# Query weights by GpSimd, one DMA for the repeated rows, and token scales broadcast without a transpose

## The chip, the cores and the metric

The kernel runs on one core of one Trainium2 chip. The metric is device time in microseconds (us), the median over runs, lower is better. The engines are named as the profile names them: PE (TensorE matmul), PEld (TensorE weight load), DVE (VectorE), ACT (ScalarE), POOL (GpSimd) and SP (SyncE, which here only issues DMAs).

## The reference, cut to what matters

64 images of 3x224x224 are cut into 64 patches of 28x28 each and projected to 128 channels; a class token and 128 text tokens are put beside them, so that a sample has L = 193 tokens of 128 channels. One attention layer and one mixture-of-experts layer follow:

```python
h = tokens(x) ++ txt                                     # 64 x 193 x 128
u = layernorm(h)
qkv = group_norm(u @ W_qkv) * scale + bias               # 8 heads, q 8, k 8, v 16 channels
logits = q.k + q.rpe_k + k.rpe_q                         # rpe: relative position, [d, i, j]
attn = softmax(logits)
h = h + group_norm(attn.v + attn.rpe_v) * scale + bias
y = layernorm(h)
top_p = two largest of softmax(y @ Wg), normalised       # 8 experts, no selection of experts
for i in range(2):                                       # every expert runs on every token
    out += sum_e gelu((y * top_p[i]) @ W1[e] + b1[e]) @ W2[e] + sum(b2)
```

The expert layer multiplies each token's hidden row by top_p[0] once and by top_p[1] once. The kernel computes `z = (y*p1) @ W1` for 32 chunks of 128 hidden units, gets the second branch as z times the ratio of the two gates, and adds the two gelus before the product with W2.

## The kernel before, in words

**Stages.** `patch_embed` writes the patch tokens to DRAM. `fused_block` then works on 32 pairs of samples (both samples side by side, T2 = 386 columns). Every engine runs the same list of steps, `SCHEDULE`, once per turn of a loop, and each engine does its own part of a step. One turn holds three pairs at once: the expert layer of pair n (32 steps `c`, of which the first three stand at the end of the turn before as `a`), the attention of pair n+1 ("late" steps), and the first norms and projections of pair n+2 (the steps in `EARLY`, up to `gaff`). A name that stands in the list after another is executed after it on every engine, in order; nothing reorders.

**One step `c` or `a`** (`mlp`): PE makes z of chunk f by three passes of 128x386 (L441, L442, L445) into one of two PSUM banks and then multiplies chunk f-3 with W2 (L432, two passes). DVE multiplies z by the ratio (L623), ACT takes two gelus (L841, L842), POOL adds them (L914, `gelu_sum`, two chunks behind PE: in step c of chunk f it adds chunk f-2). z of chunk f waits for the first gelu of chunk f-2 (two banks); L432 waits for POOL's sum; DVE's L623 waits for the sum of chunk f-4 (a ring of four buffers).

**The chain from the group norm to the logits.** `gaff`: DVE computes scale and bias of the group norm (L669 to L673), ACT writes q_f, k_f (L860) and v. SP then (`spread`, L385) writes k_f and q_f to `u_scratch` in DRAM (2 DMAs), makes the block-diagonal query weights `q_bd` by 16 DMAs from q_f (L392: for each of the 16 sample-heads its 8 partitions, the rest of q_bd stays zero from a memset in the beginning), waits for the two writes to DRAM, and reads them back eight times as `a_rep` (L395, 8 DMAs of 200 KB, partition 8*row + r holds row for r = 0 to 7). The steps `am0` to `am3` on DVE multiply a_rep by a mask into `a_bd` (L721), with one `c` between each two. `log0` to `log12` on PE take q_bd and a_bd as weights (L531, L532); log0 waits for all of q_bd and for all four masks.

**Values.** `vt0` transposes v of sample 0 of the pair on PE (L481), ACT copies it to `v_pad` (L852). There is one v_pad for both samples: `vt1` stands between the products `pv0` and `pv1` (L560), and its copy waits for pv0.

**The token scales.** For each of the two layer norms PE sums the squares per token into four columns with the token on the partition (`var1`, `var2`, L467), DVE adds epsilon (L646), POOL takes the power -0.5 (L927). In `inv1`, `inv2` PE transposes the four columns to four rows (L499) and DVE copies them out of PSUM (L649); in `bc1`, `bc2` PE broadcasts the rows over 128 partitions: weights are a column of the identity repeated 128 times, the moving side is the row (L473, `broadcast`). The two gates of the expert layer go the same way: `gate` (logits L597, maxima L776, POOL power L939), `gate2` (L781, L783), `top` (transpose L601, copy L786), `bcast` (sixteen passes of L473, then L789, L794, L796).

**GpSimd's part.** POOL executes the 32 sums, three powers and the gate's power of a turn, nothing else.

Of the kernel before, what the change touches and what calls it, by code (L numbers as in the profile page):

```python
# [39 lines left out]
P = 128  # L40
# [32 lines left out]
for _n, _w in (("ident", P), ("ones", P), ("g8", P), ("g4", P), ("mask_r", 8), ("mask_q", 8), ("place", HD + HD + HD)):  # L73
    CO[_n] = (_at, _w)
    _at += _w
# [6 lines left out]
EARLY = "txt mean1 var1 inv1 bc1 proj gmean gvar gaff".split()  # L82
OUTPUT = "w2t ot otr ocopy".split()
SCHEDULE = (
# [12 lines left out]
N_QS, N_AS = 16 * BH, 16 * 8  # L97
# [3 lines left out]
def is_first(t):  # L101
    return isinstance(t, int) and t == 0
# [161 lines left out]
def fused_block(nc, txt, w1, tok_scratch, u_scratch, out, R):  # L264

    with ExitStack() as ctx:
# [32 lines left out]
        v_pad = sb("v_pad", [P, 2, H, 32])  # L299
# [6 lines left out]
        rs1_t, ep_t = sb("rs1_t", [4, GW]), sb("ep_t", [8, GW])  # L306
        rs2_t = ep_t[0:4, :]
# [15 lines left out]
        LN = {"1": (misc, e1, e2, rs1, rs1_t), "2": (pv[0], t1, t2, rs2, rs2_t)}  # L323
# [4 lines left out]
            onorm h2_ready logits top_done dl_ready e_ready e1_ready p1_ready ep_tr ep_copied bcast_ready  # L328
# [3 lines left out]
        for k in ("1", "2"):  # L332
            for n in ("mean", "delta", "square", "var", "vareps", "rstd", "rstd_tr", "rstd_row", "rstd_bc", "x"):
                S[n + k] = sem(n + k)
# [43 lines left out]
        @block.sync  # L378
        def _(sp):
            def tokens(t, spread_free=lambda: None):  # L380
                sp.dma_start(tok[:, :, :], tok_scratch[:, bass.ds(t * 2, 2), :]).then_inc(S["tok_in"], 16)
                spread_free()
                sp.dma_start(txt_s[:, :, :], txt[bass.ds(t * 2, 2), :, :].rearrange("b t c -> t b c")).then_inc(S["tok_in"], 16)

            def spread(t):  # L385

                sp.wait_ge(S["norm"], t * 4 + 2)
                for src, x in enumerate((k_f, q_f)):
                    sp.dma_start(u_scratch[:, src, :, :], x[:, :]).then_inc(S["u_out"], 16)
# [12 lines left out]
            tokens(0)  # L402

            for piece in range(2):
                sp.dma_start(w1_st[piece].rearrange("d (e f) -> d e f", f=FF),
                             w1[4 * piece:4 * piece + 4, :, :].rearrange("e d f -> d e f")).then_inc(S["w1_in"], 16)
            for t in range(2):
                sp.wait_ge(S["h_ready"], t * 2 + 2)
                tokens(t + 1, lambda: sp.wait_ge(S["log_ready"], t * FILLS) if t else sp.wait_ge(S["setup_pool"], 1))
# [15 lines left out]
        def _(pe):  # L425
# [37 lines left out]
            def var_of(k, t):  # L463
                ps, _, sq, _, _ = LN[k]
# [19 lines left out]
            def attend(s, t):  # L484
# [11 lines left out]
                elif s in ("inv1", "inv2"):  # L496
                    pe.wait_ge(S["rstd" + s[3]], t + 1)
                    ps, _, _, rs, _ = LN[s[3]]
                    nc.tensor.transpose(ps[0:4, 0:GW], rs[0:GW, 0:4], ident[0:GW, 0:GW]).then_inc(S["rstd_tr" + s[3]], 1)  # L499
                elif s in ("bc1", "bc2"):  # L500
                    pe.wait_ge(S["rstd_row" + s[2]], t + 1)
                    ps, _, _, _, rs_t = LN[s[2]]
                    broadcast(ps, 4, 0, rs_t[:, :]).then_inc(S["rstd_bc" + s[2]], 1)
# [16 lines left out]
                elif s[:3] == "log":  # L520

                    i = int(s[3:])
                    if i == 0:
                        pe.wait_ge(S["q_spread"], t * N_QS + N_QS)
# [25 lines left out]
                elif s in ("pv0", "pv1"):  # L550
# [3 lines left out]
                    for e in range(2):  # L554
                        for c, (j0, jn) in enumerate(JC):
                            for z in range(2):
                                for j in range(H // 2):
                                    hh = 2 * j + e
                                    w = v_pad[0:jn, c, hh, :] if z == 0 else one_pad[0:jn, e, :]
# [39 lines left out]
                elif s == "top":  # L599
                    pe.wait_ge(S["p1_ready"], t + 1)  # L600
                    nc.tensor.transpose(pv[0][0:8, 0:GW], ep[0:GW, :], ident[0:GW, 0:GW]).then_inc(S["ep_tr"], 1)  # L601
                elif s == "bcast":
                    pe.wait_ge(S["ep_copied"], t + 1)
                    broadcast(pv[0], 8, 0, ep_t[:, :])
                    broadcast(pv[1], 8, 4, ep_t[:, :]).then_inc(S["bcast_ready"], 1)
# [7 lines left out]
        def _(dve):  # L613
# [66 lines left out]
            def attend(s, t):  # L680
# [13 lines left out]
                elif s in ("inv1", "inv2"):  # L694
                    layernorm("inv", s[3], t)
# [113 lines left out]
            v.memset(v_pad[:, :, :, :], 0.0).then_inc(z, 1)  # L809
# [25 lines left out]
        def _(act):  # L835
# [73 lines left out]
        def _(pool):  # L909
# [19 lines left out]
            def attend(s, t):  # L929
# [11 lines left out]
            g.memset(q_bd[:, :, :, :], 0.0).then_inc(S["setup_pool"], 1)  # L941
# [14 lines left out]
def shape_constants(np):  # L956
# [11 lines left out]
    put("g4", (p[:, None] // 4 == p[None] // 4) / 4.0)  # L968
    put("mask_r", p[:, None] // HD == np.arange(8)[None])
# [40 lines left out]
```

## Time and profile before

| | us |
|---|---|
| median of 3 runs | 3904.54 (3902.61 to 3911.96) |
| the profiled execution | 3891.26 |
| its span | 3889.4 |
| PE busy in the span | 3295.7 (85%) |
| DVE busy | 2164.7 (56%) |
| ACT busy | 1953.9 (50%) |
| POOL busy | 1197.8 (31%) |
| mean granted TensorE clock | 0.952 of full speed |

Times in rows are microseconds from the start of the span, durations of single instructions in nanoseconds where the row says so. A turn of the loop is counted here from one log0 to the next. Idle time of an engine costs only where something that ends last waits for it. A row of a timeline that ends in `[x <-E name L]` says that the engine sat idle for x us before it, until instruction L of engine E.

### The profile page before, as it was taken

What the parts mean: (1) busy time and instruction counts of PE and PEld (TensorE: products, weight loads), DVE (VectorE), ACT (ScalarE), POOL (GpSimd) and SP (SyncE); (2) the same over time, 40 slices, a digit from 0 to 9 for tenths busy, and PEclk for the clock granted to TensorE, in tenths of its full rate; (3) what the DMA queues carried; (4) which work ended last, traced back from release to release, by engine and by line L of the source; (5) the groups of instructions that cost most, each with busy time, mean ns of one, the idle gap of its engine ahead of it and who ended that gap; (6) DMA issues with size and microseconds to landing.
All of it is one profiled execution on the core that took longest, in us unless ns stands there. A gap on an engine that the chain in (4) does not pass through costs nothing.

```text
span 3889.4 us, 66829 instructions
## 1 busy us (share of the span) xinstructions
PE 3295.7 (85%) x22496; PEld 2686.9 (69%) x22496; DVE 2164.7 (56%) x4181; ACT 1953.9 (50%) x3603; POOL 1197.8 (31%) x1191
## 2 busy tenths in 40 slices
PE   4775788988888888988888889888888889888888
PEld 4664666777677666777776667776776667777776
DVE  6883455555555555555555555555555555555554
ACT  6882344544445544544455444444455445444455
POOL 0000133332333333333233333323333333323335
PEclk9997799999999999999999999999999999999999
DMA  8771111001111111001111111011111110011110
GB/s 187 153 144 49 23 25 24 12 16 22 24 22 24 24 24 24 7 19 24 24 22 24 24 24 20 9 22 24 22 24 24 24 24 9 19 22 24 22 22 5
DMA packets 263695, 124.72 MB, mean 32 GB/s; under 512 B 118494, under 2 KB 262174, under 8 KB 263326
## 3 DMA queue, kind: packets, MB, share of 16 engines
q1 hardware_dynamic: 261250, 118.87, 15.6%
q10 hardware_dynamic: 2416, 5.47, 0.4%
q8 instruction: 17, 0.28, 0.0%
q14 instruction: 12, 0.10, 0.0%
HBM read 106.03 MB, written 14.97 MB: 31 GB/s over the span
## 4 chain that ended last, share of the span: by engine, by line
issue 56%; POOL 21%; PE 10%; DVE 2%; SPq 1%; ACT 1%; POOLq 1%; DMA 0%; ACTq 0%; DVEq 0%
POOL gelu L914 20%; PE bank L432 3%; PE bank L508 1%; PE bank L473 1%; PE bank L461 1%; POOL gst L927 1%; PE bank L467 1%; SPq L392 1%; PE bank L441 1%; ACT gelu L842 1%; POOLq L913 0%; PE bank L445 0%; PE bank L442 0%; DVE gelu L623 0%; PE bank L531 0%
## 5 line engine op out<-in xcount | busy, mean ns | idle before, releaser
L914 POOL TENSOR_TENSOR gelu<-gelu 128x386 f32<-128x386 f32 x1024 | 1041.1, 1025 | 2105.8 <-ACT gelu L842 2102.2
L841 ACT ACTIVATE gelu<-bank,b_s 128x386 f32<-128x386 f32 x1024 | 595.4, 581 | 1080.9 <-DVE gelu L623 1068.5
L432 PE MATMUL bank<-gelu,w_s 128*128 128x386 f32 x2048 | 855.3, 504 | 33.6 <-POOL gelu L914 30.1
L623 DVE TENSOR_TENSOR gelu<-bank,ratio 128x386 f32<-128x386 f32 x1024 | 562.9, 555 | 475.5 <-PE bank L445 469.9
L441 PE MATMUL bank<-x_hi,w_hi 128*128 128x386 f32 x1024 | 542.9, 530 | 265.9 <-ACT gelu L841 264.6
L842 ACT ACTIVATE gelu<-gelu,b_s 128x386 f32<-128x386 f32 x1024 | 623.8, 609 | 0.0
L441 PEld LDWEIGHTS bank<-x_hi,w_hi 128*128 128x128 f32 x1024 | 196.5, 192 | 441.8 <-ACT gelu L841 353.4
L531 PE MATMUL bank<-k_f,q_bd 128*128 128x193 f32 x1600 | 405.2, 336 | 58.3 <-DVE a_bd L721 58.3
L432 PEld LDWEIGHTS bank<-gelu,w_s 128*128 128x128 f32 x2048 | 374.4, 194 | 82.3 <-POOL gelu L914 57.4
L881 ACT ACTIVATE lp<-bank,mx 128x193 f32<-128x193 f32 x800 | 292.2, 419 | 253.3 <-DVE mx L731 253.3
L731 DVE TENSOR_REDUCE mx<-bank 128x2 f32<-128x386 f32 (+1 forms) x416 | 226.4, 544 | 339.0 <-PE bank L532 336.0
L532 PE MATMUL bank<-rw,a_bd 128*128 128x193 f32 x1600 | 401.7, 334 | 0.0
L442 PE MATMUL bank<-x_hi,w_lo 128*128 128x386 f32 x1024 | 354.0, 346 | 0.0
L445 PE MATMUL bank<-x_lo,w_hi 128*128 128x386 f32 x1024 | 353.7, 345 | 0.0
L531 PEld LDWEIGHTS bank<-k_f,q_bd 128*128 128x128 f32 x1600 | 289.7, 195 | 70.0 <-issue 70.0
L574 PE MATMUL bank<-probs,rv 128*128 128x128 f32 x1600 | 309.1, 274 | 0.0
L575 PE MATMUL bank<-probs,rv 65*128 65x128 f32 x1600 | 309.1, 274 | 0.0
L744 DVE TENSOR_TENSOR lp<-bank,con 128x512 f32<-128x512 f32 (+1 forms) x224 | 139.1, 633 | 288.8 <-PE bank L575 288.8
L721 DVE TENSOR_TENSOR a_bd<-a_rep,con 128x768 f32<-128x768 f32 (+1 forms) x128 | 161.7, 1265 | 234.4 <-DMA a_rep<-u_scratch 234.4
L532 PEld LDWEIGHTS bank<-rw,a_bd 128*128 128x128 f32 x1600 | 290.9, 195 | 0.0
L887 ACT ACTIVATE probs<-bank 65x512 f32<-65x512 f32 (+1 forms) x224 | 122.3, 546 | 335.1 <-PE bank L544 335.1
L262 DVE TENSOR_TENSOR xl<-xt,xh 84x1792 fp32r<-84x1792 f32 x64 | 229.7, 3628 | 48.8 <-ACT xh L236 48.5
(145 smaller groups left out, 4942.3 us busy)
## 6 DMA issues: line engine op xcount, KB each, us to landing
a_rep<-u_scratch SPq DMA_DIRECT2D x256, 200.0 KB, 4.7
xt<-in_x SPq DMA_DIRECT2D x192, 196.0 KB
q_bd<-q_f SPq DMA_DIRECT2D x512, 6.2 KB
txt_s<-in_txt SPq DMA_DIRECT2D x32, 128.0 KB, 2.1
u_scratch<-k_f SPq DMA_DIRECT2D x32, 100.0 KB, 2.2
u_scratch<-q_f SPq DMA_DIRECT2D x32, 100.0 KB, 2.2
out<-o_s SPq DMA_DIRECT2D x64, 48.5 KB
out<-o_s SPq DMA_DIRECT2D x64, 48.0 KB
```

Source lines behind the costliest of these rows:

```text
L432: mm(yb[:, 0:T2], w2_s[:, f, :], gelu1[:, f % RING, :], start=(f == 0), stop=(f == NF - 1)).then_inc(S["w2_done"], 1)
L441: mm(z, w1_hi[:, w], x_hi[:, :], start=True, stop=False)
L442: mm(z, w1_lo[:, w], x_hi[:, :], start=False, stop=False)
L445: mm(z, w1_hi[:, w], x_lo[:, :], start=False, stop=True).then_inc(S["z_ready"], 1)
L531: mm(dst, q_bd[:, o, :, :], k_f[:, 0:L], start=True, stop=False)
L532: m = mm(dst, a_bd[:, o, :, :], rw[:, 192 - 8 * o:192 - 8 * o + L], start=False, stop=True)
L574: mm(part, rv[:, (8 * o + P) * HD:(8 * o + P) * HD + P], pr[0][:, o, :, :], start=True, stop=False)
L575: m = mm(part, rv[0:JC[1][1], 8 * o * HD:8 * o * HD + P], pr[1][0:JC[1][1], o, :, :], start=False, stop=True)
L623: v.tensor_tensor(gelu2[:, f % RING, :], zb[f % 2][:, 0:T2], ratio[:, :], ALU.mult).then_inc(S["z2_done"], 1)
L841: a(gelu1[:, f % RING, :], zb[f % 2][:, 0:T2], ACT.Gelu, bias=b1_s[:, f:f + 1]).then_inc(S["g_done"], 1)
L842: a(gelu2[:, f % RING, :], gelu2[:, f % RING, :], ACT.Gelu, bias=b1_s[:, f:f + 1]).then_inc(S["g_done"], 1)
L914: g.tensor_tensor(gelu1[:, f % RING, :], gelu1[:, f % RING, :], gelu2[:, f % RING, :], ALU.add).then_inc(S["hs_done"], 1)
```

## The change

q_bd is no longer written by DMAs. A new constant `mask_bh` [128, 16] is 1 where partition // 8 equals the sample-head, and POOL multiplies q_f by it in five steps `qs0` to `qs4` of 5 octets each (128 x 640 elements): the first three at the end of the turn before, after `otr`, `ocopy` and `hres`, the last two after the first two of the four `c` that lead the turn. log0 waits for five counts of POOL in place of 16 DMAs. `u_scratch` is laid out so that one DMA whose source repeats each row eight times writes all of a_rep. `inv1`, `inv2` and `top` are gone: `broadcast` now takes the column of token scales itself, repeated 128 times, as weights and the identity as the moving side. Each sample has its own v_pad, and `vt1` stands directly after `vt0`. The steps from `bc1` to `gate` stand closer: from the step `oaff` to `gaff` there are now 6 `c` where there were 9, and from `gaff` to `bcast` 7 where there were 4.

```diff
-EARLY = "txt mean1 var1 inv1 bc1 proj gmean gvar gaff".split()
+EARLY = "txt mean1 var1 bc1 proj gmean gvar gaff qs0 qs1 qs2".split()
 SCHEDULE = (
-    "c c c c am0 c am1 c am2 c am3 vt0 hkeep log0 log1 ... log8 "
+    "c qs3 c qs4 c c am0 c am1 c am2 c am3 vt0 vt1 hkeep log0 log1 ... log8 "
     "log9 ... log12 c c tr0 tr1 rel0 ... rel5 rel6 "
-    "c pv0 c vt1 rec0 pv1 c rec1 place0 txt place1 c c omean mean1 c ovar c var1 oaff c inv1 oh2 c bc1 mean2 c c "
-    "var2 proj c inv2 c "
-    "gmean bc2 c gvar c gate c gaff c gate2 c top c c bcast w2t xin w2t w2t ot a otr a ocopy hres a"
+    "c pv0 c rec0 pv1 c rec1 place0 txt place1 c c omean mean1 c ovar c var1 oaff c bc1 oh2 c proj mean2 c "
+    "gmean c var2 gvar c bc2 c gaff c gate c c gate2 c c c c bcast w2t xin w2t w2t ot a otr qs0 a ocopy qs1 hres a qs2"
 ).split()
...
+QS = (0, 5, 10, 15, 20, OCT)
...
-        v_pad = sb("v_pad", [P, 2, H, 32])
+        v_pad = [sb(f"v_pad{b}", [P, 2, H, 32]) for b in range(2)]
...
                 for src, x in enumerate((k_f, q_f)):
-                    sp.dma_start(u_scratch[:, src, :, :], x[:, :]).then_inc(S["u_out"], 16)
-                for bh in range(BH):
-                    rows = slice(DK * bh, DK * bh + DK)
-                    sp.dma_start(q_bd[rows, :, bh, :], q_f[rows, :].rearrange("p (o r) -> p o r", r=8)).then_inc(S["q_spread"], 16)
+                    sp.dma_start(u_scratch[src, :, :, :].rearrange("d b i -> b d i"), x[:, :]).then_inc(S["u_out"], 16)
                 sp.wait_ge(S["u_out"], t * 32 + 32)
-                for r in range(8):
-                    sp.dma_start(a_rep[r:P - 7 + r:8, :, :], u_scratch[:, :, :, :].rearrange("b s d i -> (s d) b i")).then_inc(S["a_spread"], 16)
+                sp.dma_start(a_rep[:, :, :], u_scratch[:, :, :, :].rearrange("s d b i -> (s d) (b i)").unsqueeze(1)
+                             .broadcast_to([2 * DK, 8, BH * LP])).then_inc(S["a_spread"], 16)
...
-            def broadcast(ps, rows, first, src):
+            def broadcast(ps, cols):
                 for i, a in enumerate(GO):
-                    m = mm(ps[:, a:a + GW], ident[0:rows, first + i:first + i + 1].broadcast_to([rows, P]), src,
+                    m = mm(ps[:, a:a + GW], cols[0:GW, i:i + 1].broadcast_to([GW, P]), ident[0:GW, 0:GW],
                            start=True, stop=True)
                 return m
...
             def copy_v(b, t):
                 act.wait_ge(S["vt"], t * 2 + b + 1)
-                if b == 1:
-                    act.wait_ge(S["pv_done"], t * 2 + 1)
+                if not is_first(t):
+                    act.wait_ge(S["pv_done"], t * 2 - 1 + b)
...
+                elif s[:2] == "qs":                       # POOL
+                    o0, o1 = QS[int(s[2]):int(s[2]) + 2]
+                    if s == "qs0":
+                        pool.wait_ge(S["norm"], t * 4 + 2)
+                        if not is_first(t):
+                            pool.wait_ge(S["log_ready"], t * FILLS)
+                    g.tensor_tensor(q_bd[:, o0:o1, :, :],
+                                    q_f[:, 8 * o0:8 * o1].rearrange("p (o r) -> p o r", r=8).unsqueeze(2).broadcast_to([P, o1 - o0, BH, 8]),
+                                    K["mask_bh"].unsqueeze(1).unsqueeze(3).broadcast_to([P, o1 - o0, BH, 8]), ALU.mult).then_inc(S["q_spread"], 1)
...
-            g.memset(q_bd[:, :, :, :], 0.0).then_inc(S["setup_pool"], 1)
...
-    u_scratch = nc.dram_tensor("u_scratch", (BH, 2, DK, LP), F32, kind="Internal").ap()
+    u_scratch = nc.dram_tensor("u_scratch", (2, DK, BH, LP), F32, kind="Internal").ap()
```

## Rows read from the trace of the kernel before

**Rows 1.** Waits over the span: who waited for whom, total us, times, longest us.
```profile
PE bank L441 <- ACT gelu L841: 264.6, 153, 8.5
DVE a_bd L721 <- DMA a_rep<-u_scratch: 234.4, 32, 20.1
PE bank L560 <- ACT v_pad L852: 41.4, 32, 1.3
```

**Rows 2.** Timeline of SP, 2160 to 2222: start us, us, issues.
```profile
2189.92 0.59 SPq L389 DMA_DIRECT2D u_scratch<-k_f  x1
2190.56 0.59 SPq L389 DMA_DIRECT2D u_scratch<-q_f  x1
2191.20 11.90 SPq L392 DMA_DIRECT2D q_bd<-q_f  x16
2203.22 5.14 SPq L395 DMA_DIRECT2D a_rep<-u_scratch  x8
```

**Rows 3.** DMA issues over the span: count, KB each, median us to landing.
```profile
u_scratch<-k_f SPq DMA_DIRECT2D x32, 100.0 KB, 2.2
```

**Rows 4.** Timeline of DVE, 2163 to 2222, the masks.
```profile
2206.25 0.56 DVE L623 TENSOR_TENSOR gelu<-bank,ratio 128x386 f32<-128x386 f32 x1 [0.62 <-PE bank L445]
2213.72 1.09 DVE L721 TENSOR_TENSOR a_bd<-a_rep,con 128x896 f32<-128x896 f32 x1 [6.91 <-DMA a_rep<-u_scratch]
...
2215.20 0.95 DVE L721 TENSOR_TENSOR a_bd<-a_rep,con 128x768 f32<-128x768 f32 x1
...
2216.53 1.77 DVE L721 TENSOR_TENSOR a_bd<-a_rep,con 128x768 f32<-128x768 f32 x1
...
2218.70 1.28 DVE L721 TENSOR_TENSOR a_bd<-a_rep,con 128x768 f32<-128x768 f32 x1
```

**Rows 5.** Timeline of PE, 2163 to 2222.
```profile
2187.98 0.92 PE L432 MATMUL bank<-gelu,w_s 128*128 128x386 f32 x2 [0.87 <-POOL gelu L914]
...
2190.15 0.25 PE L601 MATMUL bank<-con,ep 97*8 97x97 f32 x1
2191.23 0.45 PE L441 MATMUL bank<-x_hi,w_hi 128*128 128x386 f32 x1 [0.83 <-ACT gelu L841]
...
2208.32 0.81 PE L432 MATMUL bank<-gelu,w_s 128*128 128x386 f32 x2
2215.95 0.69 PE L441 MATMUL bank<-x_hi,w_hi 128*128 128x386 f32 x1 [6.82 <-ACT gelu L841]
...
2220.13 0.56 PE L531 MATMUL bank<-k_f,q_bd 128*128 128x193 f32 x2 [1.13 <-DVE a_bd L721]
```

**Rows 6.** Timeline of POOL, 2163 to 2222.
```profile
2195.01 1.00 POOL L914 TENSOR_TENSOR gelu<-gelu 128x386 f32<-128x386 f32 x1 [0.18 <-ACT gelu L842]
2200.53 1.00 POOL L914 TENSOR_TENSOR gelu<-gelu 128x386 f32<-128x386 f32 x1 [4.52 <-ACT gelu L842]
...
2216.48 1.01 POOL L914 TENSOR_TENSOR gelu<-gelu 128x386 f32<-128x386 f32 x1 [7.39 <-ACT gelu L842]
2217.81 1.35 POOL L914 TENSOR_TENSOR gelu<-gelu 128x386 f32<-128x386 f32 x1 [0.33 <-ACT gelu L842]
```

**Rows 7.** One line's instructions: count, duration ns min/median/max, first and last start, forms.
```profile
L914 POOL TENSOR_TENSOR gelu<-gelu x1024: 997/1009/1362, 438.6 to 3878.4; 128x386 f32<-128x386 f32 x171
L721 DVE TENSOR_TENSOR a_bd<-a_rep,con x128: 947/1094/1774, 354.5 to 3754.8; 128x768 f32<-128x768 f32 x96, 128x896 f32<-128x896 f32 x32
```

**Rows 8.** Windows: stretch, length, busy PE PEld DVE ACT POOL, granted clock, DMA share, GB/s.
```profile
1999.10:2110.90 111.80, 98.62 (x662) 80.07 (x662) 59.71 (x128) 53.57 (x112) 37.24 (x38) 0.95 0.11 21
2110.90:2220.10 109.20, 95.90 (x661) 77.32 (x662) 59.68 (x128) 53.47 (x111) 37.10 (x38) 0.97 0.11 21
460.10:3756.20 3296.10, 2895.46 (x19830) 2337.47 (x19831) 1799.81 (x3840) 1605.55 (x3301) 1114.20 (x1111) 0.96 0.11 21
1992.00:2004.00 12.00, 7.95 (x22) 6.86 (x23) 6.82 (x8) 6.02 (x12) 3.36 (x3) 0.50 0.06 15
```

**Rows 9.** Timeline of SP and then of DVE, 320 to 365: the first pair.
```profile
330.93 0.65 SPq L389 DMA_DIRECT2D u_scratch<-k_f  x1
...
354.50 3.70 DVE L721 TENSOR_TENSOR a_bd<-a_rep,con 128x896 f32<-128x896 f32 x4 [20.15 <-DMA a_rep<-u_scratch]
```

**Rows 10.** Timeline of DVE, 430 to 465: the second pair.
```profile
453.64 1.09 DVE L721 TENSOR_TENSOR a_bd<-a_rep,con 128x896 f32<-128x896 f32 x1 [8.60 <-DMA a_rep<-u_scratch]
```

More of the change, by code:

```diff
@@ L72 @@
 _at = 0
-for _n, _w in (("ident", P), ("ones", P), ("g8", P), ("g4", P), ("mask_r", 8), ("mask_q", 8), ("place", HD + HD + HD)):
+for _n, _w in (("ident", P), ("ones", P), ("g8", P), ("g4", P), ("mask_bh", BH), ("mask_r", 8), ("mask_q", 8), ("place", HD + HD + HD)):
     CO[_n] = (_at, _w)
@@ L96 @@
 FILLS = (OCT + 1) // 2
-N_QS, N_AS = 16 * BH, 16 * 8
+QS = (0, 5, 10, 15, 20, OCT)
 LOGS = 4
@@ L305, in fused_block @@
         rs1, rs2 = sb("rs1", [P, 4]), sb("rs2", [P, 4])
-        rs1_t, ep_t = sb("rs1_t", [4, GW]), sb("ep_t", [8, GW])
-        rs2_t = ep_t[0:4, :]
         x_hi = sb("x_hi", [P, T2], F32R)
@@ L321, in fused_block @@
         lt = bank[3:7]
-        LN = {"1": (misc, e1, e2, rs1, rs1_t), "2": (pv[0], t1, t2, rs2, rs2_t)}
+        LN = {"1": (misc, e1, e2, rs1), "2": (pv[0], t1, t2, rs2)}
         names = """w1_in w1_hi_ready w1_split setup_dve setup_pool setup_act tok_in txt_t h_ready qk_ready v_ready
@@ L327, in fused_block @@
             vt v_copied tr_ready tr0_copied tr1_copied wm_done pv_done pv_ready rec_done o_part obn omv omean ospread ovar ove orstd oaff_part oaffine
-            onorm h2_ready logits top_done dl_ready e_ready e1_ready p1_ready ep_tr ep_copied bcast_ready
+            onorm h2_ready logits top_done dl_ready e_ready e1_ready p1_ready bcast_ready
             xp_done ffn_in xh_done gtmp otmp rel_ready z_ready z2_done g_done hres_done h_kept hs_done w2_done ot_ready o_t os_ready out_done""".split()
@@ L332, in fused_block @@
         for k in ("1", "2"):
-            for n in ("mean", "delta", "square", "var", "vareps", "rstd", "rstd_tr", "rstd_row", "rstd_bc", "x"):
+            for n in ("mean", "delta", "square", "var", "vareps", "rstd", "rstd_bc", "x"):
                 S[n + k] = sem(n + k)
@@ L408, in _ @@
                 sp.wait_ge(S["h_ready"], t * 2 + 2)
-                tokens(t + 1, lambda: sp.wait_ge(S["log_ready"], t * FILLS) if t else sp.wait_ge(S["setup_pool"], 1))
+                tokens(t + 1, lambda: sp.wait_ge(S["log_ready"], t * FILLS) if t else None)
                 spread(t)
@@ L463, in var_of @@
             def var_of(k, t):
-                ps, _, sq, _, _ = LN[k]
+                ps, _, sq, _ = LN[k]
                 pe.wait_ge(S["square" + k], t + 1)
@@ L495, in attend @@
                     var_of(s[3], t)
[L496 to L499, printed above, removed]
                 elif s in ("bc1", "bc2"):
-                    pe.wait_ge(S["rstd_row" + s[2]], t + 1)
-                    ps, _, _, _, rs_t = LN[s[2]]
-                    broadcast(ps, 4, 0, rs_t[:, :]).then_inc(S["rstd_bc" + s[2]], 1)
+                    ps, _, _, rs = LN[s[2]]
+                    pe.wait_ge(S["rstd" + s[2]], t + 1)
+                    broadcast(ps, rs).then_inc(S["rstd_bc" + s[2]], 1)
                 elif s == "proj":
@@ L523, in attend @@
                     if i == 0:
-                        pe.wait_ge(S["q_spread"], t * N_QS + N_QS)
+                        pe.wait_ge(S["q_spread"], t * (len(QS) - 1) + len(QS) - 1)
                         pe.wait_ge(S["a_masked"], t * 4 + 4)
@@ L558, in attend @@
                                     hh = 2 * j + e
-                                    w = v_pad[0:jn, c, hh, :] if z == 0 else one_pad[0:jn, e, :]
+                                    w = v_pad[b][0:jn, c, hh, :] if z == 0 else one_pad[0:jn, e, :]
                                     m = mm(pv[b][32 * j:32 * j + 32, 256 * z:256 * z + LP], w,
@@ L598, in attend @@
                     m.then_inc(S["logits"], 1)
-                elif s == "top":
+                elif s == "bcast":
                     pe.wait_ge(S["p1_ready"], t + 1)
[L601 to L605, printed above, removed]
+                    broadcast(pv[0], ep[:, 0:4])
+                    broadcast(pv[1], ep[:, 4:8]).then_inc(S["bcast_ready"], 1)
             pe.wait_ge(S["const_in"], N_CONST)
@@ L637, in layernorm @@
                 src = h[:, :, :].rearrange("p b l -> p (b l)") if k == "1" else h2[:, :]
-                ps, delta, sq, rs, rs_t = LN[k]
+                ps, delta, sq, rs = LN[k]
                 if s == "mean":
@@ L646, in layernorm @@
                     v.tensor_scalar(rs[0:GW, 0:4], ps[0:GW, 0:4], LN_EPS, None, ALU.add).then_inc(S["vareps" + k], 1)
-                elif s == "inv":
-                    dve.wait_ge(S["rstd_tr" + k], t + 1)
-                    v.tensor_copy(rs_t[:, :], ps[0:4, 0:GW]).then_inc(S["rstd_row" + k], 1)
                 else:
@@ L693, in attend @@
                     layernorm("var", s[3], t)
-                elif s in ("inv1", "inv2"):
-                    layernorm("inv", s[3], t)
                 elif s in ("bc1", "bc2"):
@@ L719, in attend @@
                     if s == "am0":
-                        dve.wait_ge(S["a_spread"], t * N_AS + N_AS)
+                        dve.wait_ge(S["a_spread"], t * 16 + 16)
                     v.tensor_tensor(a_bd[:, o0:o1, :, :],
@@ L783, in attend @@
                     v.reciprocal(ep[0:GW, 4:8], dl[0:GW, 4:8]).then_inc(S["p1_ready"], 1)
-                elif s == "top":
-                    dve.wait_ge(S["ep_tr"], t + 1)
-                    v.tensor_copy(ep_t[:, 0:GW], pv[0][0:8, 0:GW]).then_inc(S["ep_copied"], 1)
                 elif s == "bcast":
@@ L808, in _ @@
             v.memset(half[:, 1:2], 2.718281828459045).then_inc(z, 1)
-            v.memset(v_pad[:, :, :, :], 0.0).then_inc(z, 1)
+            v.memset(v_pad[0][:, :, :, :], 0.0); v.memset(v_pad[1][:, :, :, :], 0.0).then_inc(z, 1)
             dve.wait_ge(z, 5)
@@ L845, in copy_v @@
                 act.wait_ge(S["vt"], t * 2 + b + 1)
-                if b == 1:
-                    act.wait_ge(S["pv_done"], t * 2 + 1)
+                if not is_first(t):
+                    act.wait_ge(S["pv_done"], t * 2 - 1 + b)
                 for c, (j0, jn) in enumerate(JC):
-                    blk = v_pad[0:jn, c, :, :].rearrange("p h n -> p (h n)")
+                    blk = v_pad[b][0:jn, c, :, :].rearrange("p h n -> p (h n)")
                     dst = bass.AP(tensor=blk.tensor, offset=blk.offset, ap=[list(blk.ap[0]), [64, H // 2], [32 + HD, 2], [1, HD]])
@@ L968, in shape_constants @@
     put("g4", (p[:, None] // 4 == p[None] // 4) / 4.0)
+    put("mask_bh", p[:, None] // DK == np.arange(BH)[None])
     put("mask_r", p[:, None] // HD == np.arange(8)[None])
```

2 rows, old and new, of the table SCHEDULE are left out of this document.

## The prediction

> **What bounds the kernel now.** I read the waits first. VectorE waits for a_rep in each of the 32 pairs, 234.4 us in all, and TensorE waits 264.6 us for the gelus that stand behind those masks; a third row, 41.4 us in 32 equal pieces of 1.3 us, is pv1 waiting for the copy of v [rows 1]. Then I read one turn as a timeline. SP issues the two writes of u_scratch at 2189.92, spends 11.90 us on sixteen small DMAs for q_bd, and only then issues the eight reads of a_rep, 2203.22 to 2208.4 [rows 2]. The last lands by 2213.72, where DVE has been idle 6.91 us [rows 4]. PE ran ahead as far as its two banks allow, stopped at 2209.1 and stood for 6.82 us; log0 began at 2220.13, after a further 1.13 us for the last mask [rows 5]. So the turn is bound by TensorE, except for one hole that begins in SP's queue. Turns come in two lengths, 109.2 and 111.8 us, mean 3296.1/30 = 109.87 [rows 8].
>
> **The change, part by part.** The sum is made on the profiled execution, 3891.3 us.
>
> *Transfer.* The sixteen q_bd issues (11.90 us) leave SP's queue; what follows them there is a_rep, then the stores, which only come earlier. q_f and k_f are ready three steps c earlier. A step c is 1.2 us of PE here; with the removed copies, and with VectorE's 0.9 us operations of this stretch partly in the way, I put the norm 4.6 us earlier, at 2185.3. Two issues of 0.6 us, 2.2 us for the second to land [rows 3], one issue: the single DMA starts at about 2189.4. The same 1638 KB took 2213.7 - 2203.2 = 10.5 us in eight DMAs [rows 2, 4], 156 GB/s, partly limited by 5.14 us of issuing. With 10.5 us again it lands at 2199.9, and am0 does not come up before 2206.8, the end of the sixth L623 [rows 4]. Margin 7 us: the DMA wait goes. Bounds for the transfer: 5.4 us (without the issue time) to 21 us (half the engines). Even 21 us gives 2210.4, only 0.8 us after the am0 that I find below, so this cost does not enter the sum.
>
> *What is late next: POOL.* The five products are 128x640 each. No row has that shape on POOL. The nearest is L914, 386 elements in 1.01 us, two SBUF inputs like the product [rows 7]. Below, a product could cost that 1.0 us (all fixed cost); in proportion it is 1.67 us; for the access pattern (runs of eight) I allow half as much again, 2.5 us. VectorE pays nothing for the same kind of pattern: a mask of 768 takes 0.95 us when alone [rows 4]. I take 1.6 us. qs0 and qs1 stand where POOL is idle for 4.52 us, 2196.0 to 2200.5 [rows 6]: 3.2 us and about half a microsecond behind the two-input x_lo of VectorE fit, so they cost nothing up to 2.0 us each. From 2200.5 on POOL has no cover. Until log0 it must do the sums of chunks 0 to 6 (7 x 1.0) and qs2 to qs4 (3 x 1.6 = 4.8).
>
> *The masks now collide with POOL.* Queued behind each slow sum are L432 on PE (and with it the next z), L623 on DVE four chunks later, and behind those the gelus. So am0 comes up when POOL is still three sums behind, and mask and sum meet. The rows show what happens then: a mask of 0.95 us took 1.77 and 1.28 us beside the sums at 2216.48 and 2217.81, and the second of these sums took 1.35 us [rows 4, 6]. That reads as one waiting for the other to end. I therefore add the four masks (1.09 + 3 x 0.95 = 3.9) to POOL's chain, and allow 0.35 for the hres step of VectorE that meets sum 0: 7.0 + 4.8 + 3.9 + 0.35 = 16.0, so the masks are done at 2200.5 + 16.0 = 2216.5. If they never met, the masks would follow the steps c as before: am0 at 2206.8, and from am0's start to log0 it is 6.4 us now (2213.72 to 2220.13), so 2213.2. I keep both ends and take the serial one, as every pair of rows in this stretch shows it.
>
> The Trainium skill states the same as a lock: page "SBUF — State Buffer", section "Who interferes with whom", a two-input VectorE instruction and a GpSimd instruction that reads SBUF block each other whole. By that rule log0 is at 2216.5, by free sharing at 2213.2; the trace's 1.77 us against 0.95 agrees with the rule.
>
> Another page speaks against the change: "GPSIMD Engine Reference", section 4.1, keeps elementwise products off GpSimd, about 2x slower than VectorE with two inputs. Its 4497 ns for 2048 elements would make a product 1.4 to 1.6 us, an estimate from that page; the row's 1.01 us for 386 is in line with it, and what it warns of is the 4.8 us of products in the sum above.
>
> *vt1 beside vt0.* Both use one PSUM bank, so vt1 waits for ACT to copy v of sample 0, and ACT has two gelus before it: about 0.8 us on PE behind the masks, log0 at 2217.3. What it removes is the 1.3 us before pv1 [rows 1], where nothing else is late. Stage: 2220.13 - 2217.3 = 2.8 us. pv1: 1.3 us.
>
> *Transposes.* Three go, 0.25 us of PE each [rows 5], 0.7 us with the broadcasts unchanged in columns. The tighter list from oaff to gaff is dense on VectorE. I walked it step by step and find pieces of 0.2 to 0.3 us at gvar, bc2 and the next L432, and 1.2 us on the second c after gate, where ACT is held by the four activations of gaff: about 2.0 us together. The waits that they replace are 0.87 and 0.83 [rows 5] and 0.3 before. Net nothing; bounds plus or minus 2 us.
>
> *Clock.* The granted clock is 0.50 from 1992 to 2004, after PE stood still for 6.8 us [rows 8]: that is the 1.2 GHz level. In most turns the half speed falls under the masks and costs nothing (109.2 us); where it lasts into the logits the turn takes 111.8. The new turn has no hole over 3 us, so I expect full clock and the mean falls to the short turn: (109.87 - 109.2) x 30 = 20 us.
>
> *First two pairs.* a_rep for pair 0 comes at 330.9 + 1.2 + 2.2 + 10.5 = 345 in place of 354.5 [rows 9]; POOL needs 5 x 1.6 = 8 us in parallel. Pair 1 waits 8.60 us [rows 10] and gets some 6 back. Together 15 us.
>
> Sum: 30 x (2.8 + 1.3 + 0.7) = 144, + 20 + 15 = 179. 3891.3 - 179 = 3712. The median of the runs stood 13 us above the profiled execution; part of that will be clock turns that now go. I add 4: 3716 us.
>
> **The rivals.**
>
> *A, the products or the collisions cost little.* For it: the short turn from 2206.8 on would be free. Products of 1.0 us and no collisions leave POOL out of the sum, and log0 stands at 2213.2 + 0.8 = 2214.0, a stage gain of 6.1 in place of 2.8: 3716 - 30 x 3.3 = 3617 us. Against: rows 4 and 6.
>
> *B, POOL takes half as much again, 2.5 us a product.* 3 x 0.9 + 2 x 0.5 = 3.7 us more per turn: 3716 + 111 = 3827 us. The same place goes for a worse middle stretch of 2 us together with dearer products.
>
> *C, slower: POOL becomes the bound of the turn.* The saving to be eaten is 2.8 + 1.3 + 0.7 + 35/30 = 6.0 us a turn. A product of q us costs 3(q - 1.6) + 2(q - 2.0), which passes 6.0 at q = 2.95. At q = 4 it is 11.2 us a turn, 5.2 worse than before: 3716 + 336 = 4052 us. Only the pattern of eight-element runs speaks for it; the plain L914 does not.
>
> *D, the one DMA does not spread.* The wait stays if it takes over 19 us, below 86 GB/s. At a quarter of the engines, 42 us: a_rep at 2231.4, log0 6.4 us after, at 2237.8, 17.7 us later than before, less the 2.0 us of pv1 and transposes: 3891 - 35 + 30 x 15.7 = 4327 us. Against it: the destination has 128 partitions and the source 16 rows, like the eight DMAs before.
>
> **How the numbers follow.** Forecast 0.55 (own range 3665 to 3770), A 0.20, B 0.14, C 0.06, D 0.03, no net change by the sum of B and a bad middle stretch 0.02. A difference below 0.3% is what this measurement can't tell from none. Faster: 0.55 + 0.20 + 0.13 = 0.88; same: 0.03; slower: 0.09. The range leaves out C, D and the outer parts of A and B: 3605 to 3840.
>
> **What would show it.** L721 no longer waits for the DMA; a_rep's single issue lands 5 to 12 us after its start. The product's row has 1.5 to 1.7 us. L721 has a median above 1.3 us and L432 waits for L914 two to four times a turn between bcast and log0. The clock stays at 1.00 in the turns. pv1 has no wait. A turn is 104 to 105 us. The forecast is wrong if the product is over 2 us, if the masks run at 0.95 us beside the sums, or if waits at gvar, bc2 or gate exceed 3 us a turn.

## The result, and the profile after

The changed kernel takes 3640.59 us (median of 4 runs, 3637.4 to 3644.37) against 3903.57 for the kernel before: ratio 0.9327, 95% interval 0.9304 to 0.935. I had said 3716, in a range of 3605 to 3840; the forecast's own range, 3665 to 3770, was missed by 24 us. The profiled execution has a span of 3635.6 us, 253.8 less than before.

The waits over the span of the changed kernel (who waited for whom, total us, times, longest us):

```profile
POOL gelu L893 <- ACT gelu L821: 1575.1, 334, 18.8
PEld bank L426 <- POOL gelu L893: 150.9, 220, 1.3
PE bank L435 <- ACT gelu L820: 78.2, 152, 1.0
PE bank L426 <- POOL gelu L893: 74.5, 157, 1.0
PE bank L475 <- ACT v_pad L831: 50.0, 32, 1.6
```

The wait of VectorE for a_rep in every pair (234.4 us in [rows 1]) is gone; one of 8.4 us stays in the first pair. TensorE's wait for the gelus fell from 264.6 to 78.2 us. In its place stand many short waits of TensorE for GpSimd's sums, and 1.6 us a pair before the second transpose of v.

SP's queue and the transfer, in the timeline of one turn and over the span (count, KB, median us to landing):

```profile
2144.55 0.55 SPq L386 DMA_DIRECT2D u_scratch<-k_f  x1
2145.14 0.60 SPq L386 DMA_DIRECT2D u_scratch<-q_f  x1
2147.39 0.55 SPq L388 DMA_DIRECT2D a_rep<-u_scratch  x1
```
```profile
a_rep<-u_scratch SPq DMA_DIRECT2D x32, 1600.0 KB, 9.8
```

It lands at 2157.2; the first mask runs at 2167.7. Ten microseconds of margin, where there had been a hole of 6.91 us [rows 4].

The stage from bcast to log0 in the same turn, first GpSimd (to set against [rows 6]), then VectorE's masks [rows 4], then TensorE [rows 5]:

```profile
2155.82 2.86 POOL L922 TENSOR_TENSOR q_bd<-q_f,con 128x640 f32<-128x640 f32 x2
2160.07 1.00 POOL L893 TENSOR_TENSOR gelu<-gelu 128x386 f32<-128x386 f32 x1 [1.39 <-ACT gelu L821]
2161.03 1.40 POOL L922 TENSOR_TENSOR q_bd<-q_f,con 128x640 f32<-128x640 f32 x1
2162.40 1.00 POOL L893 TENSOR_TENSOR gelu<-gelu 128x386 f32<-128x386 f32 x1
2163.36 1.29 POOL L922 TENSOR_TENSOR q_bd<-q_f,con 128x640 f32<-128x640 f32 x1
2164.61 1.00 POOL L893 TENSOR_TENSOR gelu<-gelu 128x386 f32<-128x386 f32 x1
2165.58 1.28 POOL L922 TENSOR_TENSOR q_bd<-q_f,con 128x640 f32<-128x640 f32 x1
2166.82 9.81 POOL L893 TENSOR_TENSOR gelu<-gelu 128x386 f32<-128x386 f32 x7
```
```profile
2167.72 1.08 DVE L703 TENSOR_TENSOR a_bd<-a_rep,con 128x896 f32<-128x896 f32 x1
...
2169.84 1.60 DVE L703 TENSOR_TENSOR a_bd<-a_rep,con 128x768 f32<-128x768 f32 x1
...
2171.84 1.29 DVE L703 TENSOR_TENSOR a_bd<-a_rep,con 128x768 f32<-128x768 f32 x1
...
2173.53 1.28 DVE L703 TENSOR_TENSOR a_bd<-a_rep,con 128x768 f32<-128x768 f32 x1
```
```profile
2153.55 1.92 PE L467 MATMUL bank<-con,ep 97*128 97x97 f32 x16
...
2165.67 0.92 PE L426 MATMUL bank<-gelu,w_s 128*128 128x386 f32 x2 [0.76 <-POOL gelu L893]
...
2167.88 0.92 PE L426 MATMUL bank<-gelu,w_s 128*128 128x386 f32 x2 [0.76 <-POOL gelu L893]
...
2173.12 0.38 PE L475 MATMUL bank<-con,e 128*128 128x128 f32 x2
2175.10 0.44 PE L475 MATMUL bank<-con,e 128*128 128x128 f32 x2 [1.59 <-ACT v_pad L831]
2175.37 0.49 PE L521 MATMUL bank<-k_f,q_bd 128*128 128x193 f32 x2
```

From sum 0 (2160.07) on GpSimd is never idle before log0; L426 waits for it. From bcast (2153.55) to log0 (2175.37) it is 21.8 us. In the kernel before it was 26.3, from this row to log0 at 2220.13 [rows 5]:

```profile
2193.79 2.02 PE L473 MATMUL bank<-ep_t,con 8*128 8x97 f32 x16
```

Two windows (length, busy time of PE, PEld, DVE, ACT and POOL, granted clock, DMA share, GB/s): a turn, and the turns together, against [rows 8].

```profile
2073.10:2175.40 102.30, 94.42 (x661) 75.42 (x660) 59.76 (x125) 53.75 (x110) 45.87 (x43) 1.00 0.09 22
460.00:3460.00 3000.00, 2769.78 (x19412) 2212.78 (x19410) 1735.82 (x3667) 1569.00 (x3209) 1340.47 (x1226) 1.00 0.09 22
```

A turn takes 102.3 us, and all thirty but the first (102.5) lie within 0.06 us; before the mean was 109.87. The granted clock is 1.00, the 2.4 GHz level. So the 253.8 us are 30 x 7.54 = 226 in the turns, 17 us before the first log0, 7.5 between the first two, 3 at the end. Of the 17, some 6 us lie in front of the changed part: `fused_block` starts at 302.1 in place of 308.3 in these two executions, and between 302 and 309 in those of the experiments.

### The profile page after: what moved, and what is told of

Its sections match the earlier page's. It is cut to its first block, busy times and chain, and to the rows that moved or that the text cites. A ratio compares the mean times of both kernels' runs of the same rounds, so it can differ in the third digit from the quotient of the medians.

```text
span 3635.6 us, 66086 instructions
## 1 busy us (share of the span) xinstructions
PE 3225.6 (89%) x22400; PEld 2606.3 (72%) x22400; DVE 2144.6 (59%) x4086; ACT 1961.1 (54%) x3603; POOL 1478.3 (41%) x1350
## 4 chain that ended last, share of the span: by engine, by line
issue 53%; POOL 26%; PE 11%; DVE 1%; POOLq 0%; DMA 0%; ACT 0%; DVEq 0%; SPq 0%; ACTq 0%
POOL gelu L893 19%; POOL q_bd L922 4%; PE bank L426 2%; PE bank L498 1%; POOL rs L906 1%; PE bank L467 1%; POOL gst L906 1%; PE bank L435 1%; PE bank L439 1%; PE bank L436 1%; PE bank L455 1%; PE bank L461 1%; PE bank L501 1%; PE bank L521 0%; PE bank L522 0%
## 5 line engine op out<-in xcount | busy, mean ns | idle before, releaser
L893 POOL TENSOR_TENSOR gelu<-gelu 128x386 f32<-128x386 f32 x1024 | 1113.0, 1104 | 1577.9 <-ACT gelu L821 1575.1
L426 PE MATMUL bank<-gelu,w_s 128*128 128x386 f32 x2048 | 844.9, 499 | 79.5 <-POOL gelu L893 74.5
L435 PE MATMUL bank<-x_hi,w_hi 128*128 128x386 f32 x1024 | 539.5, 527 | 79.5 <-ACT gelu L820 78.2
L426 PEld LDWEIGHTS bank<-gelu,w_s 128*128 128x128 f32 x2048 | 355.0, 189 | 169.7 <-POOL gelu L893 150.9
L521 PE MATMUL bank<-k_f,q_bd 128*128 128x193 f32 x1600 | 393.4, 328 | 10.3 <-DVE a_bd L703 10.3
L522 PE MATMUL bank<-rw,a_bd 128*128 128x193 f32 x1600 | 393.0, 328 | 0.0
L521 PEld LDWEIGHTS bank<-k_f,q_bd 128*128 128x128 f32 x1600 | 281.8, 191 | 10.7 <-issue 10.7
L522 PEld LDWEIGHTS bank<-rw,a_bd 128*128 128x128 f32 x1600 | 283.3, 190 | 0.0
L235 ACT ACTIVATE xh<-xt 84x1792 fp32r<-84x1792 f32 x64 | 230.6, 3671 | 39.9 <-DMA xt<-in_x 39.9
```

The costliest lines, as they stand in the source:

```text
L426: mm(yb[:, 0:T2], w2_s[:, f, :], gelu1[:, f % RING, :], start=(f == 0), stop=(f == NF - 1)).then_inc(S["w2_done"], 1)
L435: mm(z, w1_hi[:, w], x_hi[:, :], start=True, stop=False)
L521: mm(dst, q_bd[:, o, :, :], k_f[:, 0:L], start=True, stop=False)
L522: m = mm(dst, a_bd[:, o, :, :], rw[:, 192 - 8 * o:192 - 8 * o + L], start=False, stop=True)
L893: g.tensor_tensor(gelu1[:, f % RING, :], gelu1[:, f % RING, :], gelu2[:, f % RING, :], ALU.add).then_inc(S["hs_done"], 1)
```

## The experiments

Times are medians of four executions (six in experiment 1). The kernel before, run beside each, took 3911.17 us beside experiments 1 to 4, 3896.61 beside 6 to 9 and 3903.72 beside 5 and 10 to 12. So the ratios compare better than the times, and their intervals of 0.2 to 0.3% either way leave differences under some 15 us open. "Turn" is the mean distance from one log0 to the next over the thirty turns of the loop.

**1. One DMA for a_rep, alone.** On the kernel before:

```diff
-                for r in range(8):
-                    sp.dma_start(a_rep[r:P - 7 + r:8, :, :], ...)
+                sp.dma_start(a_rep[:, :, :], ...broadcast_to([2 * DK, 8, BH * LP]))
```

`u_scratch` and the two writes to it take the new order with it, as in the change.

> The kernel before with a_rep written by one DMA in place of eight; the sixteen q_bd DMAs stay ahead of it in SP's queue. Theory (the 11.9 us of q_bd issues are the cost): the DMA still starts at 2203.2 on the axis of before and takes the 9.8 us that the changed kernel shows, so it lands at 2213.0 in place of 2213.7, 0.7 us a turn, about 3880 us. Rival (the eight issues and their small packets are the cost): the wait shrinks by the 5.1 us of issuing, about 3750 us.

3884.11 us, ratio 0.9931 (0.991 to 0.9953). The wait for the DMA:

```profile
DVE a_bd L721 <- DMA a_rep<-u_scratch: 212.5, 32, 19.6
```

21.9 us less over 32 pairs, 0.7 each, as expected. With the sixteen issues still ahead, the eight were not what costs.

**2. Products on GpSimd, alone.** On the kernel before:

```diff
-                for bh in range(BH):
-                    ... sp.dma_start(q_bd[rows, :, bh, :], ...)
+                elif s[:2] == "qs":      # POOL, five products
+    "c qs3 c qs4 c c am0 ... otr qs0 a ocopy qs1 hres a qs2"
```

> The kernel before with q_bd made by GpSimd at the places of the change, and nothing else: eight DMAs for a_rep, transposes, one v_pad, old spacing. Theory: a_rep starts at about 2193.3 and lands at 2203.8, before am0 can run, so the DMA wait goes with this edit alone; stage 4.5 to 5 us, clock 0.7 us a turn, first pairs 15 us: 3903 - 160 - 15 = about 3725 us. Rival (one DMA or the closer spacing is needed as well): a wait of L721 for the DMA of 1 us or more stays in each turn, 3760 us or more.

3721.31 us, ratio 0.9511 (0.9482 to 0.9541); turn 104.95 us, as expected. On the kernel before, this one edit gives 4.9 of the 7.5 us a turn. The DMA wait is gone with eight DMAs and the old spacing:

```profile
DVE a_bd L719 <- DMA a_rep<-u_scratch: 9.1, 1, 9.1
PE bank L430 <- POOL gelu L912: 99.0, 176, 1.0
PE bank L558 <- ACT v_pad L850: 41.4, 32, 1.3
```

**3. Old distances between the steps.** The changed kernel with the order of before from bc1 to bcast, without the transposes:

```diff
-oaff c bc1 oh2 c proj mean2 c gmean c var2 gvar c bc2 c gaff c gate c c gate2 c c c c bcast
+oaff c oh2 c bc1 mean2 c c var2 proj c c gmean bc2 c gvar c gate c gaff c gate2 c c c bcast
```

> The changed kernel with the steps from bc1 to bcast back at their old distances (nine c between oaff and gaff, four after), still without transposes. Theory: a_rep has 10 us to spare, so the later norm costs nothing, and the closer spacing was worth nothing in itself: 3641 us, within 15. Rival (the closer spacing gained, since it let the queue run ahead of VectorE): slower by 1 to 2 us a turn, 3670 to 3700 us.

3639.84 us, ratio 0.9308 (0.9279 to 0.9337), turn 102.36. With the products on GpSimd the closer spacing is worth nothing.

**4. vt1 late, one v_pad.** The changed kernel with

```diff
-c am3 vt0 vt1 hkeep log0 ... c pv0 c rec0 pv1
+c am3 vt0 hkeep log0 ... c pv0 c vt1 rec0 pv1
```

> The changed kernel with one v_pad and vt1 back between pv0 and pv1. Theory: the 1.3 us wait before pv1 comes back, the 1.59 us wait before vt1 goes, but log0 then waits for the last mask and starts only 0.5 us earlier: 0.8 us a turn slower, about 3665 us. Rival (the two waits cancel): 3641 us, within 8.

3681.83 us, ratio 0.9415 (0.9386 to 0.9443), turn 103.6: 1.3 us a turn slower, where I had said 0.8. Its waits:

```profile
PE bank L521 <- DVE a_bd L703: 56.3, 32, 11.4
PE bank L550 <- ACT v_pad L831: 41.5, 32, 1.3
```

The wait before pv1 is back whole. The 1.59 us before vt1 had cost nothing: TensorE waits there for the last mask anyway, and the 0.4 us by which log0 is later are the transposes of vt1 themselves, which have to be done in either place.

**5. The transposes back.** Experiment 3 with inv1, inv2 and top, their copies and the old `broadcast`:

```diff
+                elif s in ("inv1", "inv2"):
+                    nc.tensor.transpose(ps[0:4, 0:GW], rs[0:GW, 0:4], ident[0:GW, 0:GW])
```

> The changed kernel with the old distances from bc1 to bcast and with inv1, inv2 and top back (three transposes on TensorE, three copies on VectorE, broadcast with the row as moving side). It differs from the kernel with the old distances alone (3640 us) by the transposes only. Theory (what the other runs leave over: products 190, v_pad 41, one DMA at most 27 of 270 us): 1.2 us a turn, about 3678 us. Rival (only the 0.25 us of TensorE time each, as I predicted): 0.7 us a turn, 3662 us.

3686.03 us, ratio 0.9441 (0.9425 to 0.9458), turn 103.69: 1.33 us more than experiment 3, as expected. Two waits are new:

```profile
PEld bank L496 <- POOL rs L924: 24.0, 33, 1.5
PEld bank L598 <- DVE ep L780: 22.9, 31, 2.3
```

That is 46.9 us, 1.5 a pair, in which a weight load stood waiting, nearly all of it under running matmuls. In the turns without a clock loss (103.3 us here, 102.2 in experiment 3), counted from the start of one matmul to the start of the next, TensorE spends 1.4 us on the three transposes where they run 0.25 us each, 0.5 us more on the broadcasts, and 0.8 us less on its other steps. That is 1.1 us; the other 0.2 of the mean lies in a few longer turns, up to 105.6 us.

**6. Three products twice.** Each of qs2 to qs4 is computed a second time on GpSimd.

```diff
+                    if s in ("qs2", "qs3", "qs4"):
+                        g.tensor_tensor(q_bd[...], ...).then_inc(S["q_twice"], 1)
+                        pool.wait_ge(S["q_twice"], ...)
```

> The changed kernel with each of qs2, qs3 and qs4 computed twice by GpSimd (the second writes the same values over the first, after a wait for it). Theory (GpSimd sets the pace from sum 0 to the last mask, a product costs 1.29 us): 3 x 1.3 to 1.4 us a turn more, 3641 + 120 = about 3761 us. Rival (the masks or TensorE set the pace and the products are hidden): 3641 to 3670 us.

3804.75 us, ratio 0.9763 (0.9732 to 0.9794), turn 107.5: 5.2 us more for 3.9 us of work and three waits. Work added to GpSimd shows in full, so GpSimd sets the pace of the stage. From bcast to log0 it is now 27.2 us, 5.3 more, so all of the loss lies there. The part above the expected 4.2 was not taken apart; the clock falls again in every turn, before log0, which fits it:

```profile
2060.00:2170.00 110.00, 99.63 (x672) 79.73 (x673) 60.63 (x127) 55.92 (x117) 48.73 (x46) 0.95 0.09 20
```

**7. Three larger products.** `QS = (0, 9, 17, OCT)`, qs3 and qs4 dropped.

> The changed kernel with three products of 9, 8 and 8 octets (1152 and 1024 elements) in place of five of 5; two stand in GpSimd's idle stretch, one behind sum 0. Theory (a fixed part of about 0.6 us, 1.1 ns an element by the rows of 386 and 640 elements): products of 1.9 and 1.7 us, 2.1 us less on GpSimd behind sum 0, of which 1.5 to 2 show: about 3590 us. Rival (the rate is 1.6 ns an element and more for larger ones): a product over 2.1 us, within 15 us of 3641.

3643.37 us, ratio 0.9351 (0.9322 to 0.9381), turn 102.4: the rival. There is no large fixed part to save, and five products or three come to the same 6.5 us:

```profile
L922 POOL TENSOR_TENSOR q_bd<-q_f,con x96: 1947/2172/3994, 327.4 to 3497.8; 128x1024 f32<-128x1024 f32 x64, 128x1152 f32<-128x1152 f32 x32
```

The 640 elements took 1.29 us, 1024 and more 2.17 in the median (columns: ns min/median/max). Behind sum 0 GpSimd does have 1.9 us less to do (one product of 2.07 us for three of 3.97), but 0.9 us of it is spent before: sum 0 starts 7.4 us after bcast instead of 6.5, behind two long products, beside which VectorE's x_lo takes 1.75 us instead of 0.87. The stage is 21.4 us instead of 21.8. Two turns in three take 101.9 to 102.1 us, the third 103.3 with a stretch at 1.2 GHz.

**8. q_bd by DMAs, behind a_rep.** The changed kernel without products; the sixteen DMAs are issued after the one of a_rep.

```diff
                 sp.dma_start(a_rep[:, :, :], ...)
+                for bh in range(BH):
+                    ... sp.dma_start(q_bd[rows, :, bh, :], q_f[rows, :]...)
```

> The changed kernel with q_bd by the sixteen DMAs again, but issued behind the one DMA of a_rep; no products on GpSimd. Theory: both land before am0 comes up, GpSimd keeps pace with the steps c, and log0 stands 6.4 us behind am0, which comes 13.0 us after bcast as in the kernel before: 2.0 us a turn faster than the change, about 3581 us. Rival (the sixteen small DMAs wait behind the large one, or log0 waits for the last of them): same or slower, 3641 or more.

3590.55 us, ratio 0.9216 (0.9187 to 0.9245), turn 100.5. As expected to 0.2 us a turn: with the DMAs in the right order GpSimd has nothing to do for q_bd, and the kernel is 43 us (by the ratios) to 50 us (by the medians) faster than the change. The stage from bcast to log0 is 19.4 us, 2.5 less than in the change: that much of the 4.0 us of products behind sum 0 had been on the path. Twelve of its thirty turns still lose 1.6 us to the clock, which is at 1.2 GHz in the first logits:

```profile
2146.10:2149.50 3.40, 3.40 (x13) 3.40 (x12) 0.56 (x1) 2.23 (x5) 1.23 (x2) 0.51 0.00 0
2046.20:2146.10 99.90, 93.56 (x661) 75.60 (x660) 58.39 (x125) 53.77 (x110) 39.47 (x38) 1.00 0.11 23
2146.10:2247.60 101.50, 95.20 (x661) 77.22 (x660) 58.35 (x125) 53.77 (x110) 39.39 (x38) 0.98 0.11 23
```

**9. q_bd by DMAs, ahead of a_rep.** As experiment 8, the loop over bh before the wait for u_scratch, as in the kernel before.

> As the kernel with the sixteen DMAs behind a_rep, but with them ahead of it, as in the kernel before; closer spacing, one DMA, one broadcast and two v_pads stay. Theory: a_rep is issued at 2157.7 on the axis of the change and lands at 2167.6, 1.0 us after am0 could run, so a short wait of about 1 us stays and there is no backlog on GpSimd: about 1 us a turn faster than the change, 3611 us. Rival (the DMA wait comes back whole, since the queue is what costs): a wait of 4 us or more and about 3720 us.

3657.97 us, ratio 0.9387 (0.9358 to 0.9417), turn 102.4. The wait is 1.4 us a turn, not 1.0, the turns vary from 101.1 to 103.9 us, and the mean granted clock is 0.973 where the change has 0.986; it comes out 47 us above my figure. Still, without the products, the rest of the change removes nearly all of the hole:

```profile
DVE a_bd L706 <- DMA a_rep<-u_scratch: 63.4, 32, 19.6
```

**10. Three products on VectorE.** qs2 to qs4 of the change move from GpSimd to VectorE, same places.

```diff
+                elif s in ("qs2", "qs3", "qs4"):     # VectorE
+                    v.tensor_tensor(q_bd[:, o0:o1, :, :], ...)
```

> The changed kernel with the three products that stand behind sum 0 (qs2 to qs4) computed by VectorE in place of GpSimd, at the same places. Theory (GpSimd's chain of sums, products and masks sets the end; VectorE has 4.5 us idle between bcast and log0 and would take 0.8 us a product): 1 to 2 us a turn faster than the change, 3580 to 3610 us. Rival (VectorE's products meet the sums as the masks do, take 1.3 to 1.6 us and push the masks back): 3641 us, within 15.

3620.31 us, ratio 0.9278 (0.9262 to 0.9293), turn 101.7. Between theory and rival: 0.7 us a turn. Most turns take 101.1 us, 1.2 less than in the change, but a third take 102.4 to 103.0, and the mean granted clock is 0.978. The products run at 0.81 us at best, 1.28 in the median beside the sums:

```profile
L703 DVE TENSOR_TENSOR q_bd<-q_f,con x96: 811/1280/1486, 325.7 to 3478.4; 128x640 f32<-128x640 f32 x96
```

**11. Masks earlier, on experiment 8.** `"c am0 c am1 c am2 c am3 c c c vt0 vt1"` in place of `"c c c c am0 c am1 c am2 c am3 vt0 vt1"`.

> q_bd by sixteen DMAs behind the one of a_rep (3590 us), and the four masks behind the first four of the seven c, so that three c follow the last one. Theory (with GpSimd free, what still ends last is the chain of masks and gelus on VectorE and ACT, during which TensorE is idle about 3 us): 2 to 3 us a turn faster, 3500 to 3530 us. Rival (a mask and a ratio step together take longer than a c and push z back, so only the last wait goes): 3560 us or more.

3570.89 us, ratio 0.9153 (0.9138 to 0.9169), turn 100.0: the fastest of all. 0.5 us a turn, not 2 to 3, so the rival holds (3560 us or more): from bcast to log0 it is 19.5 us, as in experiment 8, although log0 now starts 4.7 us after the last mask. What it gives is about the clock: every turn now takes 100.0, the good ones of experiment 8 took 99.8 to 100.0. The masks are as slow in their new place, for GpSimd again runs without a gap beside them:

```profile
2128.53 9.09 POOL L896 TENSOR_TENSOR gelu<-gelu 128x386 f32<-128x386 f32 x7 [0.69 <-ACT gelu L824]
```

**12. Masks earlier, on the change.** The same with the products left on GpSimd: `"c qs3 am0 c qs4 am1 c am2 c am3 c c c"`.

> The changed kernel, products on GpSimd as they are, with the masks behind the first four c. Theory (GpSimd's own chain of seven sums and three products stays, but no mask stands behind the last sum): 1 to 2 us a turn faster than the change, 3580 to 3610 us. Rival (the masks meet the products, which are longer than the sums, and the sum of all on the shared port is the same): 3641 us, within 15.

3699.66 us, ratio 0.9483 (0.9467 to 0.9499), turn 104.1. Both wrong: it is 59 us slower than the change. Masks and products now stand side by side, and both grow:

```profile
2091.65 1.85 POOL L893 TENSOR_TENSOR gelu<-gelu 128x386 f32<-128x386 f32 x1
2093.46 2.00 POOL L922 TENSOR_TENSOR q_bd<-q_f,con 128x640 f32<-128x640 f32 x1
...
2096.38 2.00 POOL L922 TENSOR_TENSOR q_bd<-q_f,con 128x640 f32<-128x640 f32 x1
```

A product of 1.29 us takes 2.00, a sum of 1.00 takes 1.85, and each stands in front of the sum for which L426 waits (1.00, 1.47 and 1.48 us of TensorE idle in this turn).

## Why the prediction was right, and where it was short

*The mechanism* was right: the sixteen issues of 11.9 us in SP's queue made the hole (experiments 1 and 2), the single transfer takes 9.8 us (I took 10.5), and what is late next is GpSimd (experiment 6). Three sizes were too small, the stage, the transposes and the first pairs: the forecast's saving was 188 us, the measured one 263. In one order of edits the turn's gain adds up from the parts: products 4.92 (experiment 2), vt1 1.3 (experiment 4), transposes 1.33 (experiment 5), closer spacing 0 (experiment 3), one DMA taken as 0 once the queue is short, which no run tests alone. Sum 7.55, measured 7.54; that the two agree to 0.01 is luck, since the executions of the kernel before alone differ by 17 us, over 0.5 a turn. I had 4.8 + 0.7 for the clock.

The order matters. Experiment 9 has all of the change but the products, with the sixteen issues still ahead, and its turn is 102.4 us too. So moving q_bd out of the queue and starting a_rep earlier with one DMA are two ways of closing the same hole: the first gives 4.9 us a turn on the kernel before, and nothing in the turn on top of the second. There it takes away a wait of 1.4 us and some loss of clock, and puts the products on GpSimd in their place. What the products still add is 17 us in all (3658 to 3641), most of it in the first pairs. How the second divides between the spacing and the one DMA was not run.

*Too small was the stage from bcast to log0*: 2.8 predicted, 4.5 measured. The chain from sum 0 to the end of the last mask is 14.7 us (2160.07 to 2174.81) where I had 16.0; sum 0 comes 0.2 us earlier after bcast, and log0 stands 0.6 us behind the last mask, not 0.8, of which 0.4 is work that is saved later. Of the 1.3 us in the chain the products are 0.8 (1.29 us and not 1.6). The rest is the masks: I added them whole, 3.9 us, but seven sums beside them take 9.81 us where seven free ones take 7.0, so they cost 2.8. Not all of this 1.1 shows in log0, since GpSimd has done eight sums, not the seven that I counted, when the last mask ends. Mask and sum hold each other up, but by less than the whole instruction: the two together advance in 1.7 us a step, 0.95 + 1.00 would be 1.95.

The Trainium skill (page "SBUF — State Buffer", section "Who interferes with whom") has the loser of the port that the two share fully block. The direction is what the rows of the change and experiments 11 and 12 show; for these shapes a sum loses 0.7 us to a mask of 0.95, and the measurement decides for the sum of a chain. Whether the 0.25 us less means that the port is held for only part of an instruction, no run here shows.

*Transposes*: 0.7 predicted, 1.33 measured. I counted TensorE's 0.25 us each. Each takes 0.5 us of its time, since its weights wait for GpSimd or VectorE, and the broadcasts behind them are dearer too (experiment 5).

*Clock*: 0.67 us a turn, as predicted; the new turns are equal. One reading was loose: the granted clock is at 0.50 already from 1991, inside the hole of 6.8 us (1988.15 to 1994.93), not behind it.

*First pairs*: 15 predicted, 28 measured at the two ends, of which 6 lie before the changed part and are not credited to the change.

*Signs.* The transfer (9.8 us), the clock, pv1 without a wait and the four waits of L426 came as said. The product (1.29 us, said 1.5 to 1.7), the turn (102.3, said 104 to 105) and narrowly the median of the masks (1.286 us, said above 1.3) did not.

*Rivals.* The measured time is nearer to rival A (3617) than to the forecast, and half of A's reason was right: the products are cheap. They were not free, as experiment 6 shows, and the collisions are real. B, C and D did not come. The advice against elementwise work on GpSimd ("GPSIMD Engine Reference", section 4.1, of the Trainium skill) agrees with experiment 10: with three of the products on VectorE the kernel is 20 us faster. With no product at all, and DMAs behind a_rep, it is 43 to 50 us faster (experiment 8).

## What to carry to other kernels

When a transfer is late, look first at what is issued ahead of it in its queue: with the rest of the change in place, issuing the sixteen DMAs behind the transfer gave 1.8 us a turn more than moving their work to another engine (experiment 8). On the kernel before, the reordering alone was not run. An engine that is 31% busy over the span can still set the pace of one stage; count its work there against the length of the stage, and count what it holds up on the engine beside it. A step that only moves data between layouts costs more than its length: three transposes of 0.25 us came to 1.1 us a turn at full clock. And what an edit is worth depends on what else is in place: measure it at both ends before adding parts up (experiments 2 and 9).

## What the runs showed of the hardware

- GpSimd multiplies 128x640 with two broadcast operands in 1.29 us and adds 128x386 with plain ones in 1.00.
- A short VectorE instruction can wait behind several GpSimd instructions in a row. The second row is GpSimd's, four sums without a gap; the first, 97x4 elements, ends with them. It took 2.49 us in the median of its 32 executions, 0.43 at best:

```profile
2147.17 2.49 DVE L763 TENSOR_SCALAR dl<-ep 97x4 f32<-97x4 f32 x1
```
```profile
2145.71 3.92 POOL L893 TENSOR_TENSOR gelu<-gelu 128x386 f32<-128x386 f32 x4
```

- One DMA whose source repeats each of 16 rows eight times moved 1600 KB in 9.8 us, 167 GB/s; eight DMAs of 200 KB had landed 10.5 us after the first issue.
- The granted clock fell to half in turns where TensorE had no hole over 2 us (experiment 8: waits of 0.25, 0.25 and 1.60 us before log0), and stayed full in the change with longer ones (0.76, 0.76, 0.40 and 1.59 us). What decides between the two was not settled.
